# One reciprocal of four columns per head, one head later, in an attention and expert kernel

## The chip, the cores and the metric

The kernel runs on one core of one Trainium2 chip. The metric is the device time of one execution in microseconds (us); less is better. The median of 3 runs before the change is 1390.86 us (1388.47 to 1391.62). PE is the matrix engine (TensorE), DVE VectorE, ACT ScalarE, POOL or Pool GpSimd, SP the engine that issues most transfers.

## The reference

Four sequences x of 512 rows and 512 columns. First a layer norm and a product with a quantised context of 512 x 512, added to x. Then a transformer layer with a causal attention of 16 query heads and 4 key heads of 128 columns, and a mixture of 8 experts, 2 per row. What the change touches is the softmax of the attention:

```
h = rmsnorm(hidden, attn_norm_w)
q, k, v = h @ q_w.T, h @ k_w.T, h @ v_w.T        # 16, 4 and 4 heads of 128
q, k = apply_rope(rmsnorm(q, q_norm_w)), apply_rope(rmsnorm(k, k_norm_w))
scores = einsum('bhqd,bhkd->bhqk', q, k) * scale  # then the causal mask
attn = einsum('bhqk,bhkd->bhqd', softmax(scores, axis=-1), v)
hidden = hidden + attn @ o_w.T                    # then router and experts
```

## The kernel before

Two parts run one after the other: `mixer` (norms, context product, attention, preparation of the weights; until about 1056 us) and `moe` (router and experts). The change lies in the loop of `mixer` over 16 iterations `it` (four sequences times four key heads), each with G = 4 query heads h. A head is called (it, h) here, or by its running number s = 4 * it + h. The 512 query rows of a head are four blocks q of 128 rows; because of the causal mask block q has (q + 1) * 128 keys. The four blocks of a head lie side by side in a tile `prob`, of which there are three (LAG + 1, with LAG = 2).

The way of a block: PE computes the scores (`score`, L714 and L716, three products and the mask) into one of two banks; DVE scales them and takes the row maxima (`maxima`, L1291) into `prob`; ACT takes the exponentials with the row sums in `total` (`exponentials`, L960); DVE takes the reciprocal of the sums (`invert`, L1297) into `rtotal`; then blocks 0 to 2 are multiplied with it on Pool (`normalise`, L537) and block 3 on DVE (L1302). Two heads later PE transposes prob (`transpose_p`, L724), ACT copies the result to `pT` (L966) and PE multiplies with v (`values`, L735). ACT and DVE split that result in a high and a low part (`hi_attn` L974, `lo_attn` L1308) for the output product (`output`, L752). A score waits until DVE has read its bank two blocks before (`biased`). `transpose_p(s, 0)` waits for all three of Pool's blocks and for DVE's block 3 of head s.

Between these steps each engine does other work, written out by hand in the tables FILL, FRONT, ROUTE and SPLIT_*: a slot (h, place), with place 1 to 3, names units such as 'q' and 'kv' (projection of the next iteration, L680, its rope on DVE, L1254 to L1256, and on Pool, `add_rope`, L514), 'n' (`newton`, eleven small Pool operations), 'm', 'o' (output product of the iteration before), 'cm' (`column_maxima`, L500, a partition_all_reduce on Pool over maxima that DVE takes in L1142; in slot (1, 1) of iterations 3 and 7). `units(it, h, place)` gives them in the order of the tables, and each engine runs through its part of them in order; nothing overtakes on an engine.

Per head PE runs: scores 0 and 1, the units of place 1, transposes 0 and 1 of head s - 2, score 2, the units of place 2, values and transposes 2 and 3, score 3, values, the units of place 3. Pool's order is in `normalise` and the loop behind it (L564 to L579): scalings of blocks 0 and 1, the units of place 1, the scaling of block 2, the units of places 2 and 3. The order of DVE is at L1381 to L1395. In iterations 5, 9 and 13 `add_hidden` (L505), a transfer issued by Pool, stands ahead of the first head.

Of the kernel before, what the change touches and what calls it, by code (L numbers as in the profile page):

```python
# [15 lines left out]
ALU = mybir.AluOpType  # L16
# [6 lines left out]
TT = S // P  # L23
# [3 lines left out]
G = HQ // HKV  # L27
# [140 lines left out]
NIT = B * HKV  # L168
# [8 lines left out]
LAG = 2  # L177
# [36 lines left out]
def mixer(nc, x, ctxT, w_attn, wqkvo, wexp, wx_dram, qn, kn, cos, sin, w_ffn, gate_d, ident_d, mask_d, dispf_d, ident, logits, wcolf, extra, last_acc,  # L214
# [3 lines left out]
    with ExitStack() as ctx:  # L218
        def sb(name, shape, dt=F32):
            return ctx.enter_context(nc.sbuf_tensor(name, shape, dt))  # L220

        def sem(name):
            return ctx.enter_context(nc.semaphore(name))
# [4 lines left out]
        KEYS = [(q + 1) * P for q in range(TT)]  # L228
        P_AT = [sum(KEYS[:q]) for q in range(TT)]
# [19 lines left out]
        prob = [sb(f"prob{i}", [P, sum(KEYS)]) for i in range(LAG + 1)]  # L249
# [5 lines left out]
        bias, total, rtotal = sb("bias", [P, G * TT]), sb("total", [P, G * TT]), sb("rtotal", [P, G * TT])  # L255
# [38 lines left out]
        scored, biased, exp_done, inverted = sem("scored"), sem("biased"), sem("exp_done"), sem("inverted")  # L294
        prob_ready, prob3_ready, norm_seed, norm_done, pool_own = (sem(n) for n in ("prob_ready", "prob3_ready", "norm_seed", "norm_done", "pool_own"))
# [200 lines left out]
        @block.gpsimd  # L496
        def _(pool):
            def column_maxima(f):
                pool.wait_ge(camax_done, KC * (f + 1))
                nc.gpsimd.partition_all_reduce(camaxall[:, :], camax[:, :], P, bass.bass_isa.ReduceOp.max).then_inc(callmax_done, 1)  # L500

            def add_hidden(b):
                pool.wait_ge(x1_saved, 16 * TT * (b + 1))
                pool.wait_ge(o_added, TT * HKV * (b + 1))
                pool.dma_start(out[b * S:(b + 1) * S, :].rearrange("(t p) d -> p t d", p=P), acc[b % RING_X][:, :, :], accum_op=ALU.add).then_inc(hid_added, 16)  # L505

            def add_rope(j, t):

                if j == 0:
                    pool.wait_ge(kv_rotated, t + 1)  # L510
                    nc.gpsimd.tensor_tensor(r[:, t, G * HD:R], r[:, t, G * HD:R], rot[t % 2][:, G * HD:R], ALU.add).then_inc(rope_added, 1)
                    return
                pool.wait_ge(kv_rotated, TT * j + t + 1)
                nc.gpsimd.tensor_tensor(r[:, t, :], r[:, t, :], rot[t % 2][:, :], ALU.add).then_inc(rope_added, 1)  # L514

            def add_first(t):
                pool.wait_ge(q_rotated, t + 1)
                nc.gpsimd.tensor_tensor(r[:, t, 0:G * HD], r[:, t, 0:G * HD], rot[t % 2][:, 0:G * HD], ALU.add).then_inc(first_added, 1)

            def newton(j):  # L520

                own = Steps(pool, pool_own, 1 + NEWTON_STEPS * (j - 1))
                y, half = rn[:, :, :].rearrange("p t h -> p (t h)"), ssum[:, :, :].rearrange("p t h -> p (t h)")
                pool.wait_ge(norm_seed, j + 1)
                for i in range(3):
                    own.chain(nc.gpsimd.tensor_tensor(n1[:, :], y, y, ALU.mult))
                    own.chain(nc.gpsimd.tensor_tensor(n2[:, :], n1[:, :], half, ALU.mult))
                    own.chain(nc.gpsimd.tensor_tensor(n1[:, :], n15[:, :], n2[:, :], ALU.subtract))
                    if i < 2:
                        own.chain(nc.gpsimd.tensor_tensor(y, y, n1[:, :], ALU.mult))  # L530
                nc.gpsimd.tensor_tensor(y, y, n1[:, :], ALU.mult).then_inc(norm_done, 1)
                assert own.n == NEWTON_STEPS

            def normalise(it, h, q):
                pool.wait_ge(inverted, 16 * it + 4 * h + q + 1)
                p = prob[(G * it + h) % (LAG + 1)][:, P_AT[q]:P_AT[q] + KEYS[q]]
                nc.gpsimd.tensor_tensor(p, p, rtotal[:, 4 * h + q:4 * h + q + 1].broadcast_to([P, KEYS[q]]), ALU.mult).then_inc(prob_ready, 1)  # L537

            def tables():
                pool.wait_ge(table_in, 16 * 3)  # L540
                pool.wait_ge(const_in, 16 * 6)
                pool.wait_ge(cr_ready, KC)
                nc.gpsimd.tensor_copy(mask[:, :], mask_sb[:, :])
                nc.gpsimd.memset(zero, 0.0).then_inc(table_step, 1)
                pool.wait_ge(table_step, 1)
                for n in "qk":
                    nc.gpsimd.tensor_tensor(wneg[n], zero, hrow[n][:, H:HD], ALU.subtract).then_inc(table_step, 1)
                pool.wait_ge(table_step, 3)
                c3, s3 = cos_sb.rearrange("p (t h) -> p t h", h=H), sin_sb.rearrange("p (t h) -> p t h", h=H)
                for n in "qk":  # L550
                    for a in range(2):
                        sl = slice(a * H, (a + 1) * H)
                        other = hrow[n][:, 0:H] if a else wneg[n]
                        nc.gpsimd.tensor_tensor(tab[n, "c"][:, :, sl], c3, hrow[n][:, sl].unsqueeze(1).broadcast_to([P, TT, H]), ALU.mult).then_inc(table_step, 1)
                        nc.gpsimd.tensor_tensor(tab[n, "s"][:, :, sl], s3, other.unsqueeze(1).broadcast_to([P, TT, H]), ALU.mult).then_inc(table_step, 1)

            nc.gpsimd.memset(n15[:, :], 1.5).then_inc(pool_own, 1)
            tables()
            for t in range(TT):
                add_first(t)  # L560
            for t in range(TT):
                add_rope(0, t)
            column_maxima(1)
            for it in range(NIT):  # L564
                b, g = divmod(it, HKV)
                work = {"kv": lambda t: add_rope(it + 1, t), "n": lambda _: newton(it + 1), "cm": column_maxima}
                if g == 1 and b:
                    add_hidden(b - 1)
                for h in range(G):
                    normalise(it, h, 0)  # L570
                    normalise(it, h, 1)
                    for kind, i in units(it, h, 1):
                        if kind in work:
                            work[kind](i)
                    normalise(it, h, 2)
                    for place in (2, 3):
                        for kind, i in units(it, h, place):
                            if kind in work:
                                work[kind](i)  # L579
        @block.tensor  # L580
        def _(pe):
            def transposes_x(f, t, after=None):
# [186 lines left out]
            for it in range(NIT):  # L769
# [11 lines left out]
                for h in range(G):  # L781
                    s = G * it + h - LAG
# [294 lines left out]
        def _(dve):  # L1077
# [213 lines left out]
                nc.vector.tensor_scalar(prob[(G * it + h) % (LAG + 1)][:, P_AT[q]:P_AT[q] + KEYS[q]], bank[SC + q % 2][:, 0:KEYS[q]], nscale[it % 2][:, q, h:h + 1], None,  # L1291
                                        ALU.mult, ALU.min, accum_out=bias[:, n:n + 1]).then_inc(biased, 1)

            def invert(it, h, q):
                n = 4 * h + q
                dve.wait_ge(exp_done, 16 * it + n + 1)
                nc.vector.reciprocal(rtotal[:, n:n + 1], total[:, n:n + 1]).then_inc(inverted, 1)  # L1297
                if q == TT - 1:

                    dve.wait_ge(inverted, 16 * it + n + 1)  # L1300
                    p = prob[(G * it + h) % (LAG + 1)][:, P_AT[q]:P_AT[q] + KEYS[q]]
                    nc.vector.tensor_scalar(p, p, rtotal[:, n:n + 1], None, ALU.mult).then_inc(prob3_ready, 1)  # L1302

            def lo_attn(s):
                dve.wait_ge(at_hi, s + 1)
# [58 lines left out]
            for it in range(NIT):  # L1364
# [16 lines left out]
                for h in range(G):  # L1381
                    s = G * it + h - LAG
                    maxima(it, h, 0)
                    maxima(it, h, 1)
                    invert(it, h, 0)
                    invert(it, h, 1)
                    maxima(it, h, 2)
                    fill(h, 1)
                    invert(it, h, 2)
                    maxima(it, h, 3)  # L1390
                    fill(h, 2)
                    invert(it, h, 3)
                    if s >= 0:
                        lo_attn(s)
                    fill(h, 3)  # L1395
            def part_shift():
                dve.wait_ge(xp_done, NT)
                dve.wait_ge(lg_ready, NF)
                own.chain(nc.vector.tensor_reduce(pcol[0], logits[:, 0:NF, :], AX.X, ALU.max))
                nc.vector.tensor_tensor(part[0], logits[:, 0:NF, :], wide(pcol[0]), ALU.subtract).then_inc(shifted, 1)  # L1400
# [16 lines left out]
            def part_second():  # L1417
# [5 lines left out]
                for c in range(2):  # L1423
                    nc.vector.tensor_tensor(extra[:, 0:NF, 1 + c], pcol[1 + c], pcol[3], ALU.mult).then_inc(weighed, 1)

            part_shift()
            lo_attn(G * NIT - 2)
            part_first()
# [450 lines left out]
```

## Time and profile before

| | |
|---|---|
| median of 3 runs | 1390.86 us (1388.47 to 1391.62) |
| profiled execution | 1391.31 us, span 1389.5 us |
| mean granted clock of PE | 0.966 |
| PE busy | 1255.7 us, 90% |
| DVE busy | 842.7 us, 61% |
| ACT busy | 715.9 us, 52% |
| POOL busy | 384.9 us, 28% |
| L537, Pool's scalings | 192, 119.2 us busy, 626 ns each in the mean |
| L1291, DVE's maxima | 256, 134.9 us busy |

Busy times are those of one execution, whose own time is the one beside its span. A row of a timeline gives start, duration, engine, line, operation, output and inputs, the number of instructions merged into the row, and in square brackets the idle time before it with what ended it. "issue" stands where no releaser is seen. Times in the rows count from the start of the span.

### The profile page before, as it was taken

What the parts mean: (1) busy time and instruction counts of PE and PEld (TensorE: products, weight loads), DVE (VectorE), ACT (ScalarE), POOL (GpSimd) and SP (SyncE); (2) the same over time, 40 slices, a digit from 0 to 9 for tenths busy, and PEclk for the clock granted to TensorE, in tenths of its full rate; (3) what the DMA queues carried; (4) which work ended last, traced back from release to release, by engine and by line L of the source; (5) the groups of instructions that cost most, each with busy time, mean ns of one, the idle gap of its engine ahead of it and who ended that gap; (6) DMA issues with size and microseconds to landing.
All of it is one profiled execution on the core that took longest, in us unless ns stands there. A gap on an engine that the chain in (4) does not pass through costs nothing. (4 is left out here: it accounts for less than half of the span.)

```text
span 1389.5 us, 22860 instructions
## 1 busy us (share of the span) xinstructions
PE 1255.7 (90%) x6845; PEld 1012.8 (73%) x6845; DVE 842.7 (61%) x2480; ACT 715.9 (52%) x2290; POOL 384.9 (28%) x545
## 2 busy tenths in 40 slices
PE   1777899999999999989999999999996499999995
PEld 0466667778776777777767777878775498899995
DVE  7678776767886786578768665666644422222221
ACT  6447665565674566476656646556543033333331
POOL 0223121214322132322223233332210124333331
PEclk9988999999999999999999999999998699999998
DMA  3270335432355466738445664855304788877433
GB/s 99 75 283 28 121 107 183 174 129 92 152 165 178 161 212 200 250 113 243 166 158 188 209 204 151 264 194 184 104 4 133 277 318 218 247 211 205 77 62 38
DMA packets 89894, 228.50 MB, mean 164 GB/s; under 512 B 12272, under 2 KB 50032, under 8 KB 79536
## 3 DMA queue, kind: packets, MB, share of 16 engines
q1 hardware_dynamic: 63712, 184.03, 37.7%
q0 software_dynamic: 10848, 24.71, 9.8%
q10 hardware_dynamic: 15216, 18.30, 3.7%
q8 instruction: 60, 0.98, 0.3%
q14 instruction: 58, 0.48, 0.1%
HBM read 146.76 MB, written 80.24 MB: 163 GB/s over the span
## 5 line engine op out<-in xcount | busy, mean ns | idle before, releaser
L537 POOL TENSOR_TENSOR prob<-prob,rtotal 128x128 f32<-128x128 f32 (+2 forms) x192 | 119.2, 626 | 405.3 <-DVE rtotal L1297 379.0
L960 ACT ACTIVATE prob<-prob,bias 128x128 f32<-128x128 f32 (+3 forms) x256 | 145.1, 567 | 155.1 <-DVE prob L1291 154.3
L1291 DVE TENSOR_SCALAR_CACHE_REDUCE prob<-bank,nscale 128x128 f32<-128x128 f32 (+3 forms) x256 | 134.9, 546 | 147.1 <-PE bank L716 146.8
L735 PE MATMUL bank<-pT,v 128*128 128x512 f32 (+3 forms) x512 | 175.8, 445 | 9.0 <-ACT pT L966 8.3
L680 PE MATMUL bank<-w_hi,hT_hi 128*128 128x512 f32 x480 | 173.4, 361 | 4.1 <-DVE rot L1256 4.0
L966 ACT ACTIVATE pT<-bank 128x512 f32<-128x512 f32 (+3 forms) x256 | 102.9, 432 | 130.0 <-PE bank L724 129.8
L680 PE MATMUL bank<-w_hi,hT_lo 128*128 128x512 f32 x480 | 162.2, 338 | 0.0
L680 PE MATMUL bank<-w_lo,hT_hi 128*128 128x512 f32 x480 | 162.0, 337 | 0.0
L1602 PE MATMUL gu<-we,xT_hi 128*128 x624 | 156.5, 332 | 3.2 <-DVE xT_lo L1718 2.7
L514 POOL TENSOR_TENSOR r<-r,rot 128x640 f32<-128x640 f32 x60 | 99.3, 1655 | 196.1 <-DVE rot L1256 196.1
L714 PE MATMUL bank<-kT_hi,qT_hi 128*128 128x128 f32 (+3 forms) x256 | 101.8, 397 | 20.8 <-DVE prob L1291 20.8
L1602 PEld LDWEIGHTS gu<-we,xT_hi 128*128 128x128 f32 x624 | 109.3, 190 | 9.9 <-issue 7.9
L724 PEld LDWEIGHTS bank<-ident,prob 128*128 128x128 f32 x640 | 79.0, 143 | 47.6 <-issue 33.5
L752 PE MATMUL bank<-w_hi,aT_hi 128*128 128x512 f32 x256 | 107.4, 420 | 1.6 <-issue 1.6
L1580 POOL DMA_INDIRECT out<-y,ids x39 | 61.8, 1585 | 165.3 <-ACT y L1663 116.1
L724 PE MATMUL bank<-ident,prob 128*128 128x128 f32 x640 | 103.6, 277 | 0.0
L680 PEld LDWEIGHTS bank<-w_hi,hT_hi 128*128 128x128 f32 x480 | 91.9, 191 | 15.6 <-DVE rot L1256 8.0
L1602 PE MATMUL gu<-we,xT_lo 128*128 x312 | 101.8, 326 | 0.0
L752 PE MATMUL bank<-w_lo,aT_hi 128*128 128x512 f32 x256 | 101.3, 396 | 0.0
L752 PE MATMUL bank<-w_hi,aT_lo 128*128 128x512 f32 x256 | 101.2, 395 | 0.0
L735 PEld LDWEIGHTS bank<-pT,v 128*128 128x128 f32 x512 | 86.0, 193 | 20.4 <-ACT pT L966 8.7
L680 PEld LDWEIGHTS bank<-w_hi,hT_lo 128*128 128x128 f32 x480 | 91.0, 190 | 10.6
(312 smaller groups left out, 2852.9 us busy)
## 6 DMA issues: line engine op xcount, KB each, us to landing
w_hi<-ws_scratch SPq DMA_DIRECT2D x24, 1024.0 KB, 5.2
w_lo<-ws_scratch SPq DMA_DIRECT2D x24, 1024.0 KB, 7.8
we<-wx_scratch SPq DMA_DIRECT2D x16, 1408.0 KB
we<-wx_scratch SPq DMA_DIRECT2D x16, 768.0 KB, 10.9
stage<-in_wexp SPq DMA_DIRECT2D x64, 176.0 KB, 2.4
wx_scratch<-ehi ACTq DMA_DIRECT2D x64, 176.0 KB, 2.0
wx_scratch<-stage SPq DMA_DIRECT2D x64, 176.0 KB, 2.5
stage<-in_wqkvo SPq DMA_DIRECT2D x40, 256.0 KB, 3.6
```

Of the source, the lines that this page charges most:

```text
L514: nc.gpsimd.tensor_tensor(r[:, t, :], r[:, t, :], rot[t % 2][:, :], ALU.add).then_inc(rope_added, 1)
L537: nc.gpsimd.tensor_tensor(p, p, rtotal[:, 4 * h + q:4 * h + q + 1].broadcast_to([P, KEYS[q]]), ALU.mult).then_inc(prob_ready, 1)
L680: last = nc.tensor.matmul(o, hT[a][:, k, t * P:(t + 1) * P], wkv(j, c, k) if kv else wq(j, c, k), start=(k == 0 and n == 0), stop=(k == KC ...
L714: nc.tensor.matmul(o[:, 0:KEYS[q]], qT[a][:, h, q * P:(q + 1) * P], kT[it % 2][c][:, 0:KEYS[q]], start=(n == 0), stop=False)
L724: last = nc.tensor.transpose(bank[PT + j % 2][:, (q - j) * P:(q - j + 1) * P], prob[s % (LAG + 1)][:, P_AT[q] + j * P:P_AT[q] + (j + 1) * ...
L735: nc.tensor.matmul(bank[PV][:, j * P:S], v[it % (LAG + 1)][:, j, :], pT[:, PT_AT[j]:PT_AT[j] + QS[j]], start=(j == 0), stop=(j == TT - 1)) ...
L752: last = nc.tensor.matmul(bank[t % 2][:, :], aT[a][:, (G * o + h) % RING_A, t * P:(t + 1) * P], wo(c, h), start=(h == 0 and n == 0), stop= ...
L960: nc.scalar.activation(p, p, ACT.Exp, bias=bias[:, 4 * h + q:4 * h + q + 1], scale=-1.0, accum_out=total[:, 4 * h + q:4 * h + q + 1]).then ...
L966: nc.scalar.activation(pT[:, PT_AT[j]:PT_AT[j] + QS[j]], bank[PT + j % 2][:, 0:QS[j]], ACT.Copy).then_inc(pt_copied, 1)
L1291: nc.vector.tensor_scalar(prob[(G * it + h) % (LAG + 1)][:, P_AT[q]:P_AT[q] + KEYS[q]], bank[SC + q % 2][:, 0:KEYS[q]], nscale[it % 2][:, ...
L1580: pool.indirect_dma_start(out, bass.IndirectOffsetOnAxis(ap=ids[:, i:i + 1], axis=0), y[i % 3][:, :], None, compute_op=ALU.add).then_inc(y ...
L1602: last = nc.tensor.matmul(gu[i % 2][u][:, 0:I], xT[a][i % 2][:, k, :], we[:, bass.ds(at + (c * ECOLS + k * GU + u * I), I)], start=(k == 0 ...
```

## The change

DVE takes the reciprocals of a head's four row sums in one operation of four columns, in the head after, behind its maxima 1; the scaling of block 3 goes with it. Pool's three scalings of a head move to the head after as well, in the same places of the order. The last head is handled behind the loop.

```diff
@@ Pool, loop over the heads
                 for h in range(G):
-                    normalise(it, h, 0)
-                    normalise(it, h, 1)
+                    s = G * it + h - 1
+                    if s >= 0:
+                        normalise(s // G, s % G, 0)
+                        normalise(s // G, s % G, 1)
                     for kind, i in units(it, h, 1):
                         if kind in work:
                             work[kind](i)
-                    normalise(it, h, 2)
+                    if s >= 0:
+                        normalise(s // G, s % G, 2)
                     for place in (2, 3):
                         for kind, i in units(it, h, place):
                             if kind in work:
                                 work[kind](i)
+            for q in range(TT - 1):
+                normalise(NIT - 1, G - 1, q)
@@ DVE
-            def invert(it, h, q):
-                n = 4 * h + q
-                dve.wait_ge(exp_done, 16 * it + n + 1)
-                nc.vector.reciprocal(rtotal[:, n:n + 1], total[:, n:n + 1]).then_inc(inverted, 1)
-                if q == TT - 1:
-
-                    dve.wait_ge(inverted, 16 * it + n + 1)
-                    p = prob[(G * it + h) % (LAG + 1)][:, P_AT[q]:P_AT[q] + KEYS[q]]
-                    nc.vector.tensor_scalar(p, p, rtotal[:, n:n + 1], None, ALU.mult).then_inc(prob3_ready, 1)
+            def invert(s):
+                it, h = divmod(s, G)
+                n, q = 4 * h, TT - 1
+                dve.wait_ge(exp_done, 4 * s + TT)
+                nc.vector.reciprocal(rtotal[:, n:n + TT], total[:, n:n + TT]).then_inc(inverted, TT)
+                dve.wait_ge(inverted, 4 * s + TT)
+                p = prob[s % (LAG + 1)][:, P_AT[q]:P_AT[q] + KEYS[q]]
+                nc.vector.tensor_scalar(p, p, rtotal[:, n + q:n + q + 1], None, ALU.mult).then_inc(prob3_ready, 1)
@@ DVE, loop over the heads
                     maxima(it, h, 0)
                     maxima(it, h, 1)
-                    invert(it, h, 0)
-                    invert(it, h, 1)
+                    if G * it + h:
+                        invert(G * it + h - 1)
                     maxima(it, h, 2)
                     fill(h, 1)
-                    invert(it, h, 2)
                     maxima(it, h, 3)
                     fill(h, 2)
-                    invert(it, h, 3)
                     if s >= 0:
                         lo_attn(s)
                     fill(h, 3)
@@ DVE, behind the loop
+            invert(G * NIT - 1)
             part_shift()
             lo_attn(G * NIT - 2)
             part_first()
```

## Rows read from the trace of the kernel before

**Rows 1.** The page, busy time of each engine (share of the span), instructions.
```profile
PE 1255.7 (90%) x6845; PEld 1012.8 (73%) x6845; DVE 842.7 (61%) x2480; ACT 715.9 (52%) x2290; POOL 384.9 (28%) x545
```
**Rows 2.** Waits of PE, 92 to 1045 us: total us, times, longest.
```profile
PE bank L714 <- DVE prob L1291: 20.8, 20, 4.3
...
PE bank L704 <- DVE kT_lo L1313: 5.8, 3, 5.2
PE bank L680 <- DVE rot L1256: 4.0, 10, 0.6
PE bank L634 <- DVE logits L1232: 3.8, 3, 2.2
```
**Rows 3.** Lines L1297 and L1302: duration ns minimum/median/maximum.
```profile
L1297 DVE RECIPROCAL rtotal<-total x256: 146/164/167, 94.1 to 1037.7; 128x1 f32<-128x1 f32 x128
L1302 DVE TENSOR_SCALAR prob<-prob,rtotal x64: 485/487/1590, 104.0 to 1037.9; 128x512 f32<-128x512 f32 x64
```
**Rows 4.** Timeline of DVE, maxima 3 to scaling of head (5,2).
```profile
430.61 0.75 DVE L1291 TENSOR_SCALAR_CACHE_REDUCE prob<-bank,nscale 128x512 f32<-128x512 f32 x1 [3.98 <-PE bank L716]
...
436.10 0.15 DVE L1297 RECIPROCAL rtotal<-total 128x1 f32<-128x1 f32 x1
436.29 0.49 DVE L1302 TENSOR_SCALAR prob<-prob,rtotal 128x512 f32<-128x512 f32 x1
```
**Rows 5.** Timeline of PE, score 2 of head (5,3).
```profile
440.62 0.45 PE L714 MATMUL bank<-kT_hi,qT_hi 128*128 128x384 f32 x1 [1.70 <-DVE prob L1291]
```
**Rows 6.** Timeline of DVE, maxima 1 of head (15,0).
```profile
997.25 0.48 DVE L1291 TENSOR_SCALAR_CACHE_REDUCE prob<-bank,nscale 128x256 f32<-128x256 f32 x1
```
**Rows 7.** Timeline of PE, transposes in head (15,1).
```profile
1003.47 0.94 PE L724 MATMUL bank<-ident,prob 128*128 128x128 f32 x7
```
**Rows 8.** Timeline of DVE, last output addition in the loop.
```profile
1040.46 0.69 DVE L1318 TENSOR_TENSOR last_acc<-bank,last_acc 128x512 f32<-128x512 f32 x1 [1.29 <-PE bank L752]
```
**Rows 9.** Timeline of PE, transposes of the last head.
```profile
1044.40 0.93 PE L724 MATMUL bank<-ident,prob 128*128 128x128 f32 x7
```
**Rows 10.** Timeline of Pool, `add_hidden` in iteration 5.
```profile
387.80 1.59 POOL L505 DMA_DIRECT2D out<-last_acc  x1 [4.40 <-DVE last_acc L1318]
```
**Rows 11.** Timeline of Pool around the reduction of iteration 3.
```profile
294.51 1.12 POOL L537 TENSOR_TENSOR prob<-prob,rtotal 128x128 f32<-128x128 f32 x2 [3.42 <-DVE rtotal L1297]
296.79 1.57 POOL L514 TENSOR_TENSOR r<-r,rot 128x640 f32<-128x640 f32 x1 [1.16 <-DVE rot L1256]
304.50 0.39 POOL L500 PARTITION_ALL_REDUCE camaxall<-camax  x1 [6.14 <-issue]
312.75 0.82 POOL L537 TENSOR_TENSOR prob<-prob,rtotal 128x384 f32<-128x384 f32 x1 [7.86 <-issue]
```
**Rows 12.** Timeline of DVE, the maxima that the reduction waits for.
```profile
296.62 2.28 DVE L1142 TENSOR_REDUCE camax<-cb 128x16 f32<-128x2048 f32 x1
```
**Rows 13.** Timeline of PE, transposes in heads (3,2) and (3,3).
```profile
305.66 0.93 PE L724 MATMUL bank<-ident,prob 128*128 128x128 f32 x7
...
318.28 0.93 PE L724 MATMUL bank<-ident,prob 128*128 128x128 f32 x7
```
**Rows 14.** Timeline of Pool around the reduction of iteration 7.
```profile
546.21 0.39 POOL L500 PARTITION_ALL_REDUCE camaxall<-camax  x1 [6.58 <-issue]
554.01 0.86 POOL L537 TENSOR_TENSOR prob<-prob,rtotal 128x384 f32<-128x384 f32 x1 [7.41 <-issue]
```
**Rows 15.** Timeline of PE, transposes in head (7,2).
```profile
548.30 0.93 PE L724 MATMUL bank<-ident,prob 128*128 128x128 f32 x7
```
**Rows 16.** Windows: us, busy PE, PEld, DVE, ACT, POOL, granted clock, DMA.
```profile
145.00:148.50 3.50, 1.06 (x6) 1.07 (x6) 2.97 (x6) 2.41 (x6) 0.00 (x0) 0.52 1.00 412
148.50:152.00 3.50, 3.50 (x19) 3.41 (x18) 1.81 (x8) 2.51 (x7) 0.86 (x2) 0.50 1.03 386
```
**Rows 17.** Timeline of PE, one matmul of L752 at each clock.
```profile
436.17 0.39 PE L752 MATMUL bank<-w_hi,aT_hi 128*128 128x512 f32 x1
...
443.73 0.63 PE L752 MATMUL bank<-w_lo,aT_hi 128*128 128x512 f32 x1
```

## The prediction

> **What bounds the kernel now.** I read the busy shares first: PE 90%, DVE 61%, POOL 28% [rows 1]. DVE and Pool, on which the change works, are therefore no bound by themselves; their work counts only where PE waits for it. The second view is the list of PE's waits in the attention loop (92 to 1045 us) [rows 2]. The reader is to see how little there is to win: 20.8 us in 20 waits of a score matmul (L714) for DVE's maxima, 5.8 for kT_lo, 4.0 for rot, 3.8 for the logits, and not one wait of a transpose of prob (L724). So the scaled prob is always there in time today, and the question is whether it still is when it comes a head later.
>
> **What it removes.** Per head, three of four one-column reciprocals, 256 x 164 ns before [rows 3], 64 after (I price a four-column one like a one-column one: the issue of such a tiny operation dominates; the bounds are 0.16 and twice that, nothing either way). That is 192 x 0.16 = 31 us of DVE time, and the waits for the exponentials of the same head go too. The scaling of block 3 (0.487 us) stays, but moves from behind `fill(h, 2)` to behind `maxima(h+1, 1)`. What of this PE feels is read in the streak before a typical wait [rows 4]: DVE runs without a break from maxima 3 of head (5,2) to maxima 0 of head (5,3), and in this streak lie one reciprocal and the scaling; from 436.10 to the end of the scaling at 436.78 they take 0.7; where the streak holds a second reciprocal, 0.9. PE had stood for 1.70 and starts at 440.62 as soon as DVE's block 0 is through [rows 5]. Behind the change such a wait is 0.7 to 0.9 shorter. Of the 20 waits ten are 0.66 us or longer and make 16.2 of the 20.8; one of them is ACT's doing, which leaves 9 x 0.7 = 6.3; the ten short ones lose little (1); the waits for rot and the logits lie behind the same DVE work and give perhaps 1.5. What is late next is ACT's `hi_attn`, which `lo_attn` waits for anyway, and ACT's dequantisation. Sum -8.8; I take **-8**, since one DVE streak serves several waits in a row. Bounds: -2 (only the clearest three) and -14 (all of L704 and L634 too).
>
> Between maxima 1 and maxima 2 little changes: today DVE takes two reciprocals there and stands for the exponentials ahead of each; afterwards one reciprocal and the scaling fill 0.7. I take 0; bounds -0.2 and +0.7 per head of DVE time, which PE feels only in the waits priced above. Nothing is queued behind `exp_done` there that was not before, since the exponential of block 3 of the previous head is long through.
>
> **What it adds: a head less of slack, and a place in Pool's queue.** Pool scales blocks 0 to 2 of head s now in head s+1, and PE reads all of prob(s) in head s+2, behind place 1. In an ordinary head that is enough: Pool's first scaling in head (3,1) starts at 294.51, after the change that is head (3,0)'s, and PE reads it at 305.66 [rows 11, 13], 11.1 us later, while the scalings take 1.12 and 0.82 and one rope addition 1.57. The tightest are the last two iterations: maxima 1 of head (15,0) starts at 997.25 and PE transposes at 1003.47 [rows 6, 7], 5.7 us behind its end, for a need of 0.16 + 1.12 + 0.82 and perhaps 0.5 that Pool waits beside DVE's scaling, 2.6. At the end DVE's last `invert` stands behind the output addition that starts at 1040.46 and lasts 0.69 [rows 8], so it runs at about 1041.2, Pool is through by 1043.8, and PE wants it at 1044.40 [rows 9]. Cost 0; bounds 0 and 1.5. `add_hidden` now stands ahead of the previous head's scalings in Pool's queue, with 1.59 us [rows 10] against over 10 of slack; its wait for `o_added` ends ahead of the reciprocal that the scaling waits for. Nothing on SP's queue moves.
>
> One place is different. In slot (1,1) of iterations 3 and 7 Pool also has `column_maxima`, the partition_all_reduce, and it stands **between the scalings of blocks 0, 1 and of block 2**. Follow Pool in iteration 3 [rows 11]: rope addition at 296.79, then 6.14 idle ("issue", no releaser), the reduction at 304.50, which lasts 0.39, then 7.86 idle, again "issue", and at 312.75 the scaling of block 2. DVE's maxima of the context that feed it end at 298.90 (296.62 + 2.28) [rows 12]. So Pool is shut for 13.9 us. Today the block behind it belongs to head (3,1), read at 318.28, so the hole is hidden with 4.7 to spare. After the change it is block 2 of head **(3,0)**, and PE turns to that head's prob at 305.66 [rows 13]. Pool is done at 312.75 + 0.82 = 313.6. PE, with some 0.1 for the signal, stands for **8.0 us**. In iteration 7 the reduction is at 546.21 and the scaling at 554.01 + 0.86 = 554.9 [rows 14], PE's transposes at 548.30 [rows 15]: **6.7 us**. The hole itself doesn't move, since DVE and ACT feed it from before the stall. It is PE that stops, and all that it computes is needed, so 14.7 are lost. From the second some 0.7 may come back, as the wait for the logits just behind it (the longest of [rows 2], 2.2) arises from Pool's backlog beside DVE. I take **+14**; bounds 11 and 16. Behind each stall nothing else is late: Pool catches up while PE stands.
>
> The clock. A wait of 5.2 us [rows 2] ends at 147.4 (148.5 less the 1.06 us busy); the granted clock is 0.52 in 145.0 to 148.5 and 0.50 in 148.5 to 152.0 [rows 16], its lower level of 1.2 GHz, so 4.6 us after work resumed were at half clock. A matmul of 512 columns then takes 0.63 in place of 0.39 [rows 17]: a microsecond there loses between 0.38 (by these durations) and 0.5 (by the two levels). Two stalls of this kind lose 2 x 4.6 x 0.44 = **+4**; bounds +1 and +9 (twice the stretch). Some half-clock stretches behind the short waits may go; I take -0.5 for them, bounds 0 and -4.
>
> **Sum.** -8 + 14 + 4 - 0.5 = +9.5. The profiled execution took 1391.3 (span 1389.5), 0.4 above the median of 1390.86. So 1391.3 + 9.5 = 1400.8 for such an execution, 1400.4 for the median: slower by 0.7%.
>
> **Rivals.** *A: Pool isn't shut after the reduction.* The page says that spans on POOL are rough, and the 7.86 behind the reduction have no releaser. If they were the tail of something that today's order happens to allow, block 2 could be scaled as soon as the reduction is through. The point from which it decides: block 2 of head (3,0) starts before about 305. Then there is no stall, and no half clock behind one: 1391.3 - 8 - 0.5 = 1382.8. For it: nothing in the trace names what Pool does there. Against it: the next instruction had all it needed long before, twice, with nearly the same idle time (7.86 and 7.41) [rows 11, 14]. Chance 0.05.
> The Trainium skill's page "GPSIMD Engine Reference", section "Instruction dispatch", says that the first call of a freshly loaded kernel pays about 6 us of code load. By that alone the hole would be 6 us once and PE would hardly stand; the trace agrees for the way in (298.90 to 304.50), but shows a second, longer hole on the way back, and the measured hole decides.
>
> *B: DVE and Pool get in each other's way.* The scaling of block 3 takes 487 ns at the median and 1590 at most [rows 3], the long ones beside a Pool operation already running. After the change it runs each time beside Pool's first scaling. If each pays 1.10, the 0.85 that a late head saves at best turns into 0.25 lost, and 20 waits grow by 5 us in place of shrinking by 8: 1391.3 + 14 + 4 + 5 = 1414. Against it: DVE starts the scaling 0.19 behind the start of the reciprocal [rows 4], while Pool must first see the signal, so DVE should be first and Pool pay. Chance 0.08. The Trainium skill's "GPSIMD Engine Reference", section "Key points", states that Pool shares its SBUF interfaces with DVE and names the two-port mode; it doesn't say who waits.
>
> *C: the relief is the larger part.* DVE's streaks shorten so much that ACT and PE run closer (-14) and half-clock stretches go (-4), with the stalls at their lower bound (+11) and short clock loss (+3): 1391.3 - 4 = 1387. Chance 0.04.
>
> *D: the stalls are hidden or halved* (Pool reaches the reduction earlier since DVE is less loaded): +7, +2, -8: 1392. Against it: what the reduction waits for lies in the same head on DVE, behind PE's own scores, so it comes forward no more than PE does. Chance 0.05.
>
> **Chances.** The forecast 0.78. Its own spread: low -13 + 12 + 1 - 1 = -1, high -3 + 16 + 9 = +22, but not all at once: +3 to +17. With B at +23 the range is 1393 to 1409; it leaves out A, C, D and half of B, 0.18. Slower by over 0.2% (2.8 us, about what a measurement of this kernel tells from no change): 0.77 + 0.08 = 0.85; within 0.2%: D and 0.01 of the forecast's lower end, 0.06; faster: A and C, 0.09.
>
> **What would show it.** Right: PE waits of 6 to 8 us before L724, released by Pool's L537, in iterations 3 and 7, and none elsewhere; the granted clock at half behind them; Pool's block 2 of heads (3,0) and (7,0) directly behind the 7 to 8 us hole; PE's waits for L1291 down from 20.8 to 12 or so; DVE busy down by some 31. Wrong: no L724 wait, or L1302 with a median well over 0.5 (B), or L1291 waits unchanged or under 8.

## The result, and the profile after

The changed kernel takes 1401.42 us at the median of 7 runs (1396.8 to 1405.42), the kernel before 1390.86 (1388.47 to 1391.89, 7 runs): ratio 1.0079, 95% interval 1.0066 to 1.0093, so 9 to 13 us slower. The forecast was 1400.4, in a range of 1393 to 1409. The profiled execution of the changed kernel has a span of 1400.4 us, 10.9 above that of before.

The first row to read is the busy time of each engine on the profile's page, against [rows 1]:

```profile
PE 1256.0 (90%) x6845; PEld 1012.9 (72%) x6845; DVE 829.9 (59%) x2288; ACT 716.8 (51%) x2290; POOL 392.7 (28%) x545
```

DVE has 192 instructions and 12.8 us less, and the kernel is slower all the same. PE's waits (92 to 1060 us of the changed kernel; total, times, longest) answer to [rows 2]; line numbers have moved by five, behind `invert` by four:

```profile
PE bank L719 <- DVE prob L1296: 19.5, 18, 5.6
PE bank L729 <- POOL prob L537: 14.8, 2, 7.8
PE bank L740 <- ACT pT L971: 7.4, 10, 2.5
PE bank L709 <- DVE kT_lo L1317: 5.5, 2, 5.3
PE bank L685 <- DVE rot L1261: 3.0, 7, 0.6
PE bank L757 <- issue: 1.6, 1, 1.6
PE bank L639 <- DVE logits L1237: 1.2, 3, 0.4
```

The second row is new: PE's transposes of prob wait for Pool, twice, 14.8 us in all. Every other total is the same or smaller: over the same window all rows of before sum to 45.4 us and all of these, with two more of 0.6 and 0.5, to 54.1, so the other waits fell by 6.1 (the logits 2.6, the maxima 1.3, rot 1.0, pT 0.9, kT_lo 0.3). Where the two new waits are is in Pool's timeline around the reduction of iteration 3 (answers to [rows 11]) and of iteration 7 ([rows 14]):

```profile
295.69 1.16 POOL L537 TENSOR_TENSOR prob<-prob,rtotal 128x128 f32<-128x128 f32 x2 [3.55 <-DVE rtotal L1303]
298.20 1.57 POOL L514 TENSOR_TENSOR r<-r,rot 128x640 f32<-128x640 f32 x1 [1.36 <-DVE rot L1261]
305.61 0.39 POOL L500 PARTITION_ALL_REDUCE camaxall<-camax  x1 [5.83 <-issue]
314.14 0.82 POOL L537 TENSOR_TENSOR prob<-prob,rtotal 128x384 f32<-128x384 f32 x1 [8.14 <-issue]
...
555.06 0.67 POOL L500 PARTITION_ALL_REDUCE camaxall<-camax  x1 [6.76 <-issue]
563.27 0.82 POOL L537 TENSOR_TENSOR prob<-prob,rtotal 128x384 f32<-128x384 f32 x1 [7.54 <-issue]
```

and PE starts as soon as block 2 is scaled (timeline of PE, to [rows 13, 15]):

```profile
315.01 1.76 PE L729 MATMUL bank<-ident,prob 128*128 128x128 f32 x7 [7.78 <-POOL prob L537]
...
564.14 1.75 PE L729 MATMUL bank<-ident,prob 128*128 128x128 f32 x7 [7.02 <-POOL prob L537]
```

The seven transposes take 1.76 in place of 0.93 us, at a granted clock of 0.50: PE comes back at its lower level. Windows behind the two stalls (us, busy PE, PEld, DVE, ACT, POOL, granted clock, DMA share, GB/s):

```profile
315.00:319.60 4.60, 4.59 (x20) 4.28 (x21) 1.70 (x5) 2.83 (x12) 3.17 (x4) 0.50 0.00 0
319.60:323.00 3.40, 3.40 (x18) 2.22 (x17) 0.37 (x2) 1.18 (x5) 0.00 (x0) 1.00 0.51 134
...
564.10:568.80 4.70, 4.66 (x20) 4.35 (x21) 1.77 (x5) 3.19 (x13) 3.21 (x4) 0.50 0.00 0
```

PE is busy throughout at half clock, 4.6 and 4.7 us, as behind the 5.2 us wait of [rows 16]. Yet PE's busy time over the whole kernel is that of before, 1256.0 against 1255.7 us, with as many matmuls. Half clock has gone elsewhere. The kernel before has, among others, three such stretches at about 442, 561 and 814 us (they fill most of these windows, not all):

```profile
440.00:444.00 4.00, 3.38 (x12) 2.71 (x13) 3.46 (x12) 3.40 (x11) 2.46 (x8) 0.77 0.87 294
560.00:564.00 4.00, 2.76 (x14) 2.60 (x15) 1.92 (x8) 1.07 (x2) 2.89 (x12) 0.70 0.98 406
814.00:818.00 4.00, 3.87 (x16) 3.53 (x17) 1.42 (x6) 1.87 (x5) 2.62 (x11) 0.57 0.98 402
```

In the changed kernel the clock is full in the same work a little later (450 to 458 and 824 to 832 us), the one at 561 has given way to the one behind the stall, and one is new at 248. In steps of 1 us from 92 to 1045, PE worked 26 us at half clock before and 25 after.

DVE's side shows in the wait that the prediction followed, [rows 4, 5]. Timeline of PE in the changed kernel, score 2 of head (5,3):

```profile
451.16 0.45 PE L719 MATMUL bank<-kT_hi,qT_hi 128*128 128x384 f32 x1 [1.12 <-DVE prob L1296]
```

1.70 has become 1.12. The scaling of block 3 (duration in ns, minimum/median/maximum, to [rows 3]) has got longer, the reciprocal of four columns hardly, against 164 ns for one column:

```profile
L1303 DVE RECIPROCAL rtotal<-total x64: 166/172/177, 108.5 to 1050.1; 128x4 f32<-128x4 f32 x64
L1306 DVE TENSOR_SCALAR prob<-prob,rtotal x64: 485/727/1129, 108.7 to 1050.3; 128x512 f32<-128x512 f32 x64
```

### The profile page after: what moved, and what is told of

It reads as the page before. It is cut to its first block and busy times, and to the rows that moved or that the text cites. A ratio compares the mean times of both kernels' runs of the same rounds, so it can differ in the third digit from the quotient of the medians.

```text
span 1400.4 us, 22732 instructions
## 1 busy us (share of the span) xinstructions
PE 1256.0 (90%) x6845; PEld 1012.9 (72%) x6845; DVE 829.9 (59%) x2288; ACT 716.8 (51%) x2290; POOL 392.7 (28%) x545
## 5 line engine op out<-in xcount | busy, mean ns | idle before, releaser
L537 POOL TENSOR_TENSOR prob<-prob,rtotal 128x128 f32<-128x128 f32 (+2 forms) x192 | 126.6, 683 | 273.1 <-DVE rtotal L1303 257.5
L719 PE MATMUL bank<-kT_hi,qT_hi 128*128 128x128 f32 (+3 forms) x256 | 101.6, 397 | 19.8 <-DVE prob L1296 19.5
L729 PE MATMUL bank<-ident,prob 128*128 128x128 f32 x640 | 104.8, 279 | 14.8 <-POOL prob L537 14.8
```

The lines of the kernel that those rows point to most:

```text
L719: nc.tensor.matmul(o[:, 0:KEYS[q]], qT[a][:, h, q * P:(q + 1) * P], kT[it % 2][c][:, 0:KEYS[q]], start=(n == 0), stop=False)
L729: last = nc.tensor.transpose(bank[PT + j % 2][:, (q - j) * P:(q - j + 1) * P], prob[s % (LAG + 1)][:, P_AT[q] + j * P:P_AT[q] + (j + 1) * ...
```

## The experiments

The kernels were timed in three groups, each beside its own executions of the kernel before: the first four rows, the next four, the last three. Ratios are to those, with 95% intervals; the last column is the difference of the medians. Across groups only ratios are compared. The lists of waits and busy times are of one profiled execution each.

| kernel | median us | before us | ratio | difference |
|---|---|---|---|---|
| block 2 first | 1377.73 | 1388.45 | 0.9918 (0.9897 to 0.9939) | -10.7 |
| only the reduction moved | 1382.96 | 1388.45 | 0.9962 (0.9948 to 0.9976) | -5.5 |
| Pool a head later only | 1409.39 | 1388.45 | 1.0142 (1.0122 to 1.0163) | +20.9 |
| third reduction | 1407.08 | 1388.45 | 1.0124 (1.0101 to 1.0147) | +18.6 |
| before, reduction late | 1394.23 | 1387.61 | 1.0044 (1.0029 to 1.0060) | +6.6 |
| scaling 3 behind maxima 2 | 1382.22 | 1387.61 | 0.9953 (0.9940 to 0.9966) | -5.4 |
| four reciprocals | 1377.90 | 1387.61 | 0.9926 (0.9913 to 0.9940) | -9.7 |
| copy for the reduction | 1379.39 | 1387.61 | 0.9937 (0.9924 to 0.9950) | -8.2 |
| scaling 3 behind maxima 3 | 1391.60 | 1389.69 | 1.0014 (1.0003 to 1.0026) | +1.9 |
| block 2 first, again | 1376.79 | 1389.69 | 0.9912 (0.9893 to 0.9931) | -12.9 |
| changed kernel, again | 1397.31 | 1389.69 | 1.0058 (1.0038 to 1.0079) | +7.6 |

**Take Pool's block 2 out from behind the hole.** On Pool, in the changed kernel:

```diff
+                    if s >= 0:
+                        normalise(s // G, s % G, 2)
                     for kind, i in units(it, h, 1):
                         if kind in work:
                             work[kind](i)
-                    if s >= 0:
-                        normalise(s // G, s % G, 2)
```

> The changed kernel, but Pool scales block 2 ahead of the units of place 1 in every head, so neither the reduction nor a rope addition stands between the scaling of a head and PE's reading of it. My theory (the loss is two stalls of PE, 7.8 and 7.0 us, behind the reduction's hole, plus the half clock behind them, and DVE's relief of some 5 us is real): no wait of L724 for Pool, 1401.4 - 14.8 - 3 = 1383 to 1387, faster than the kernel before by 4 to 7 us. Rival B (DVE and Pool in each other's way, scaling of block 3 at 727 ns in place of 487): the time stays above 1395 though the stalls are gone. Rival 'relief is nothing': 1390 to 1392.

0.9918, and 0.9912 in the third group: the fastest kernel of all here. Timeline of Pool in iteration 3: all three blocks, then the rope addition, then a hole as before.

```profile
296.10 1.94 POOL L537 TENSOR_TENSOR prob<-prob,rtotal 128x128 f32<-128x128 f32 x3 [3.51 <-DVE rtotal L1303]
298.61 1.56 POOL L514 TENSOR_TENSOR r<-r,rot 128x640 f32<-128x640 f32 x1 [0.57 <-DVE rot L1261]
306.22 0.39 POOL L500 PARTITION_ALL_REDUCE camaxall<-camax  x1 [6.06 <-issue]
315.37 1.55 POOL L514 TENSOR_TENSOR r<-r,rot 128x640 f32<-128x640 f32 x1 [8.76 <-DVE rot L1261]
```

PE's transposes are there at 307.49 without a wait. With the stalls the loss is gone, and the price of rival B is out. But the gain is 10.7 us, where I expected 4 to 7. This edit moves two things from ahead of block 2, the hole and the rope addition; the next kernel takes them apart.

**Move only the reduction.** In the changed kernel the units of place 1 run in their old place, except 'cm', which comes behind block 2:

```diff
-                    for kind, i in units(it, h, 1):
-                        if kind in work:
+                    held = [(kind, i) for kind, i in units(it, h, 1) if kind in work]
+                    for kind, i in held:
+                        if kind != "cm":
                             work[kind](i)
                     if s >= 0:
                         normalise(s // G, s % G, 2)
+                    for kind, i in held:
+                        if kind == "cm":
+                            work[kind](i)
```

> The changed kernel, but only the reduction of slot (1,1) in iterations 3 and 7 is moved behind the scaling of block 2; the rope additions stay ahead of it. If only the hole costs: the same as the kernel with block 2 first in every head, within 1.5 us (1383 to 1387). If the order of rope addition and block 2 matters to DVE (which waits for rope additions) the two differ by 2 us or more.

0.9962. Against the changed kernel's 1.0079 the two holes cost 1.2% or 16 us, against the 1.0058 of its second measurement 13 (forecast 18). Against the kernel with block 2 first it is 5.2 us slower: the rope addition ahead of block 2 costs too. One place is to be seen in iteration 2, head (2,1), of the changed kernel, which has the same order there. Pool's timeline, then DVE's:

```profile
238.61 1.57 POOL L514 TENSOR_TENSOR r<-r,rot 128x640 f32<-128x640 f32 x1 [1.50 <-DVE rot L1261]
240.13 0.83 POOL L537 TENSOR_TENSOR prob<-prob,rtotal 128x384 f32<-128x384 f32 x1
```
```profile
238.85 1.36 DVE L1181 TENSOR_SCALAR var<-mv 128x4 f32<-128x4 f32 x1
240.25 0.75 DVE L62 TENSOR_SCALAR t<-var 128x4 uint32<-128x4 uint32 x1
```

Two operations on 4 columns end just behind the end of a Pool operation each (240.18 and 240.96): they seem to wait for it. With block 2 first the second one doesn't:

```profile
242.87 0.17 DVE L62 TENSOR_SCALAR t<-var 128x4 uint32<-128x4 uint32 x1
```

and the wait of PE behind it is 0.47 in place of 1.06 us. Summed over PE's waits in the loop, without the row "issue", the profiles differ by 4.8 us (38.9 and 34.1). The spans of these two executions differ by 2.0 only, since PE's busy time is 1.6 lower in the slower one (1251.7 and 1253.3), so how the 5.2 us come about is shown in part.

**Pool later, DVE as before.** This is the kernel before with Pool's loop of the change; DVE's code is untouched.

> The kernel before, with Pool's scalings a head later as in the change, but DVE's four reciprocals and its scaling of block 3 where they were. My theory: both stalls (about 8.0 and 6.7 us) and the half clock behind them, without DVE's relief: 1390.9 + 14 + 3.5 = 1406 to 1410, that is 5 to 8 us above the changed kernel, and PE's waits for maxima at 19 to 21 us. If DVE's relief is worth nothing: 1401, as the changed kernel. If the change's DVE part costs (rival B): below 1400.

1.0142, and 1409.39 us lies in the expected range. It has the same two stalls, of 7.4 and 5.3 us, and none of DVE's relief. PE's waits for maxima are 23.5 us, above the 19 to 21 that I expected (PE's waits in its loop):

```profile
PE bank L719 <- DVE prob L1296: 23.5, 20, 6.2
PE bank L729 <- POOL prob L537: 12.7, 2, 7.4
```

The changed kernel lies under it by 0.6% (1.0079) to 0.8% (1.0058) of the kernel before: with Pool a head later, DVE's part of the change gains 9 to 12 us.

**One more stall.** In the changed kernel, on Pool behind the units of place 1:

```diff
+                    if (it, h) == (11, 1):
+                        nc.gpsimd.partition_all_reduce(camaxall[:, :], camax[:, :], P, bass.bass_isa.ReduceOp.max)
```

> The changed kernel with one more partition_all_reduce in slot (1,1) of iteration 11, whose result nobody reads. My theory: a third stall there. Pool's hole of 13.4 to 13.9 us begins at the end of the rope addition; from the rows of the kernel before PE would stand 5 to 6 us, and 1.5 to 2.5 us go to the half clock: 1401.4 + 7.5, range +5 to +9. If a stall is absorbed by waits further on: under +3.

1.0124, that is 6.2 us over the changed kernel by its first ratio and 9 by its second. PE's timeline:

```profile
821.31 1.76 PE L731 MATMUL bank<-ident,prob 128*128 128x128 f32 x7 [5.73 <-POOL prob L537]
```

The stall is paid. Of its half clock (4.2 us of work behind it) the totals can't say so much: in the profiles the spans differ by 6.6, PE's waits for Pool by 5.2, the other waits fall by 2.8, and PE's busy time grows by 5.0, more than the 2 us or so that this stretch costs. Half clock came up in other places too.

**Control: the reduction late in the kernel before.**

```diff
-                    for kind, i in units(it, h, 1):
-                        if kind in work:
+                    held = [(kind, i) for kind, i in units(it, h, 1) if kind in work]
+                    for kind, i in held:
+                        if kind != "cm":
                             work[kind](i)
                     normalise(it, h, 2)
+                    for kind, i in held:
+                        if kind == "cm":
+                            work[kind](i)
```

> Control: the kernel before, with the reduction of slot (1,1) moved behind that head's scaling of block 2 and nothing else. My theory: the hole is hidden in the kernel before in either order, so 0, within 2 us of it. If the hole cost something there already (Pool's backlog beside DVE, the wait for the logits), up to 3 us faster.

A miss: 1.0044, slower by 6.6 us. In the kernel before, block 2's reciprocal comes late in the head. So the hole begins at 300.2 (299.39 + 0.83), and it is longer here (Pool's timeline):

```profile
299.39 0.83 POOL L537 TENSOR_TENSOR prob<-prob,rtotal 128x384 f32<-128x384 f32 x1 [2.51 <-DVE rtotal L1301]
306.16 0.39 POOL L500 PARTITION_ALL_REDUCE camaxall<-camax  x1 [5.94 <-issue]
318.44 1.56 POOL L514 TENSOR_TENSOR r<-r,rot 128x640 f32<-128x640 f32 x1 [11.88 <-issue]
```

Behind it stand two rope additions and `newton`, whose result DVE needs for k, and PE's turn to wait comes later:

```profile
327.71 1.54 PE L708 MATMUL bank<-ident,r 128*128 128x128 f32 x6 [3.19 <-DVE r L1289]
```

This wait and the 3.0 us of half clock behind it make some 4.7 us (an estimate: 3.2 and half of 3.0); the spans of the profiled executions differ by 4.1. So the hole holds up two users, prob and k, and in the kernel before neither of them made PE wait. The rest of the 6.6 us is open.

**Where the scaling of block 3 stands.** In the kernel with block 2 first, the reciprocal stays behind maxima 1, the scaling goes behind maxima 2:

```diff
                         invert(G * it + h - 1)
                     maxima(it, h, 2)
+                    if G * it + h:
+                        scale3(G * it + h - 1)
```

> The kernel with block 2 first, and DVE's scaling of block 3 behind maxima 2 in place of ahead of it. In the changed kernel that scaling takes 727 ns at the median where it took 487, beside Pool's scalings. If DVE is held up there where PE waits: 1 to 3 us faster than the kernel with block 2 first. My theory: that place is not on PE's path, so within 1 us of it, whatever the median of the scaling becomes.

A miss: 0.9953 against 0.9918 and 0.9912, so 5 to 6 us slower than with block 2 first. In the profiles PE's waits in the loop are 2.7 us more, in many small ones. PE's busy time is 1.7 more, with a stretch of half clock (3.4 us) at 248 that the changed kernel has too and the one with block 2 first has not. What makes these waits I did not trace.

In these two kernels `invert` issues the reciprocal alone, `scale3` the scaling. The scaling behind maxima 3 instead, in the stretch in which DVE is late:

```diff
                     maxima(it, h, 3)
+                    if G * it + h:
+                        scale3(G * it + h - 1)
                     fill(h, 2)
```

> The kernel with block 2 first, and DVE's scaling of block 3 (still a head later) behind maxima 3, that is back in the stretch between maxima 3 and maxima 0 in which DVE is late for PE. My theory (DVE's relief is the 0.5 us scaling and the reciprocals out of that stretch): PE's waits for maxima and logits grow by 0.5 each in nine to eleven places, so 4 to 6 us slower than the kernel with block 2 first in this call, waits for maxima back to 20 us or so. If the place of the scaling is nothing and only the waits for exponentials counted: within 1 us of it.

> The kernel with block 2 first once more, as the yardstick of this call: 0.992 of the kernel before, 0.990 to 0.994, PE's waits for maxima at 16 to 18 us.

1.0014 against 0.9912 in the same group: 14.8 us, three times what I expected. PE's waits in its loop; the kernel with block 2 first has 16.4 in 18, 2.4 in 7 and no other row that differs by more than 0.7:

```profile
PE bank L719 <- DVE prob L1296: 22.0, 20, 6.0
PE bank L685 <- DVE rot L1261: 8.3, 19, 1.0
```

I had counted nine to eleven waits for maxima and logits; twelve more waits for rot appear, nine more than the kernel before has (10, [rows 2]). The place is not quite the old one, which may be why: in the kernel before the scaling stood behind `fill(h, 2)`, with rot's products ahead of it, here it stands in front of them. DVE in head (2,1) of the kernel before:

```profile
247.30 0.41 DVE L1256 TENSOR_TENSOR rot<-bank,tab_q_s 128x256 f32<-128x256 f32 x1
247.63 0.15 DVE L1297 RECIPROCAL rtotal<-total 128x1 f32<-128x1 f32 x1
247.82 0.49 DVE L1302 TENSOR_SCALAR prob<-prob,rtotal 128x512 f32<-128x512 f32 x1
```

So the 14.8 us are the price of this place, and what the old one costs by itself no kernel here shows. And this kernel's scaling is the quick one:

```profile
L1309 DVE TENSOR_SCALAR prob<-prob,rtotal x64: 476/483/726, 113.4 to 1042.5; 128x512 f32<-128x512 f32 x64
```

487 ns in the mean, where it is 700 with block 2 first: 14 us less of DVE work, and 14.8 us more of time. The place decides here, not the duration.

**Merging or moving.** In the kernel with block 2 first:

```diff
-                nc.vector.reciprocal(rtotal[:, n:n + TT], total[:, n:n + TT]).then_inc(inverted, TT)
+                for c in range(TT):
+                    nc.vector.reciprocal(rtotal[:, n + c:n + c + 1], total[:, n + c:n + c + 1]).then_inc(inverted, 1)
```

> The kernel with block 2 first, but four reciprocals of one column in place of one of four, at the same place a head later. It separates the merging from the moving. My theory: the three extra ones (some 0.1 to 0.2 us each, 20 to 38 us of DVE in all) lie between maxima 1 and 2 where PE seldom waits: +0 to +2 us. If the number of DVE instructions is what counts: +5 us or more, nearly all of the 10.7 us gain given back.

0.9926 against 0.9918 and 0.9912. The intervals overlap: one reciprocal of four columns is worth 0 to 2 us, and the rest of the gain is the move to the next head.

**No reduction, same place.** In the changed kernel `column_maxima` of iterations 3 and 7 becomes a copy. This leaves out the maximum over the partitions.

```diff
-                nc.gpsimd.partition_all_reduce(camaxall[:, :], camax[:, :], P, bass.bass_isa.ReduceOp.max).then_inc(callmax_done, 1)
+                nc.gpsimd.tensor_copy(camaxall[:, :], camax[:, :]).then_inc(callmax_done, 1)
```

> The changed kernel, but in iterations 3 and 7 Pool copies its input of the reduction instead of reducing it over the partitions, in the same slot and order (this leaves out the maximum over the partitions, so the scales of the context differ). It tells whether it is the hole around the reduction and not a Pool operation in that place as such. My theory: no wait of L729 for Pool, 15 to 18 us faster than the changed kernel, that is 5 to 7 us faster than the kernel before, as with the reduction moved. Rival: the place in the queue is enough to stall PE; then 5 us faster than the changed kernel at most.

0.9937, which is 17 to 20 us under the changed kernel, and no wait of PE for Pool. A Pool operation in that place of the queue makes no stall without the hole. By the medians it is 3.5 us faster than with the reduction moved (the intervals just touch). A reason fits: PE's wait for the logits, 1.82 in iteration 7 of that kernel, is 0.41 here, and the half clock behind it (0.55 in 556.3 to 560.0 there) is full clock here.

**The changed kernel once more.**

> The changed kernel once more in the same call: 1.0079 of the kernel before, 1.0065 to 1.0093, so 21 to 24 us above the kernel with block 2 first; two waits of PE for Pool of 7 to 8 us.

1.0058 (1.0038 to 1.0079), a little under the first measurement and under what I expected; the intervals overlap. The two stalls are 7.9 and 6.0 us, the second again under the expected 7 to 8. The median lies 20.5 us above the kernel with block 2 first in the same group.

## Why the prediction was right

The path that makes the kernel slower, the two stalls, was right. The terms of the sum were less so, and that it came out within 2 us is in part luck: errors of opposite sign cancel. In the profiled executions (span 10.9 us above before):

| term | forecast | in the profiles |
|---|---|---|
| DVE's relief, as waits of PE | -8 | -6.1 |
| two stalls | +14 | +14.8 |
| half clock, behind the stalls and elsewhere | +4 - 0.5 | +0.3 (PE's busy time) |
| not in the waits of the loop | 0 | +1.9 |
| sum | +9.5 | +10.9 |

**The stalls.** 8.0 and 6.7 us were forecast, 7.78 and 7.02 measured, in the two heads that were named, and no other head waits for Pool. Over the nine stalls of the four profiled executions that have them they were 5.3 to 7.9. That they are the cause is shown by the kernel in which only the reduction moved and by the one with the copy. In the first PE's only wait for Pool is 0.3 us, in the second there is none. The third reduction adds one.

**The clock.** +4 was forecast for 4.6 us at the lower level behind each stall, and 4.6 and 4.7 were measured; behind all nine it was 4.0 to 5.7, with no order by the length of the wait (5.7 behind one of 6.0, 4.6 behind one of 7.8). The step that failed is the other term: the half-clock stretches behind short waits were to give back 0.5 (bounds 0 and -4). PE's busy time grew by 0.3, so they gave back nearly all of the 4. How much of that is the change's doing stays open, since such stretches differ between kernels that are otherwise close: PE's busy time is 1251.7 with the reduction moved, 1247.6 with the copy, and 1253.3 and 1252.5 in two executions with block 2 first.

**DVE's relief.** -8 was taken from bounds -2 and -14. The pairs give -5.5 (reduction moved against before) and -9 to -12 (changed against Pool-later-only), so the size is about right. Its place is not. The row for maxima was to fall from 20.8 to 12 or so and went to 19.5, nearly unchanged, which the prediction had named as a sign of being wrong. The largest part is the logits' (3.8 to 1.2 us), which it had priced at 1.5 together with rot. Five of the long waits for maxima did shrink by about 0.6 (1.70 to 1.12 here), but others grew: the long one of head (0,2) went from 4.34 to 5.64 though PE's score came 0.65 earlier, and one at 600 us from 1.08 to 1.67. A wait's length says when the waiting engine came, too. The count of waits was also off: eleven are 0.66 us or longer and make 18.0 us, not ten with 16.2; the one left out (1.87 at 93.65) did not shrink.

What I got wrong in it is the sort of gain. I priced it by waits that existed. With the scaling between maxima 3 and rot's products the kernel takes 14.8 us more for half a microsecond per head, much of it in waits for rot that weren't there. And merging the reciprocals, the 31 us of DVE work that I wrote down, is worth 0 to 2 us. DVE's busy time fell by 12.8 only. By the sums of single durations the reciprocals fell by 30.2 (41.2 to 11.0), the scaling grew by 6.3 (38.4 to 44.7) and some small operations by the rest, 20.6 less in all (950.1 to 929.5). Neighbouring operations overlap, and the busy time (842.7 to 829.9) counts an overlap once.

**Ends of slack.** The last two iterations and the end of the loop cost nothing, as forecast: no transpose waits there, and PE's last waits of the loop are those of before.

**The rivals.** A (no second half of the hole) is out: it was 6.9 to 11.9 us long behind every reduction in iterations 3, 7 and 11. B was half right as a mechanism and wrong in its price: the scaling does get longer beside Pool (487 to 727 ns at the median, the second of the prediction's signs of being wrong that came up; 600 to 698 in the mean). But it does so between maxima 1 and 2, and the kernel in which it is quick again in the other place is the slower one. C and D fall with the measured stalls. The Trainium skill's figure of about 6 us of code load at the first call of a freshly loaded kernel (page "GPSIMD Engine Reference", section "Instruction dispatch") agrees with the 5.8 to 6.9 us from Pool's last operation to the reduction in iterations 3, 7 and 11 of all profiled kernels. Here it is paid each time, not once, and what the page doesn't state is the way back. The 13.9 us of the prediction begin at the end of DVE's maxima; the load doesn't seem to wait for them, as the rows at the end of this document show.

## What to carry to other kernels

When a step is moved by one turn of a loop, follow it past every rare item in each queue, not only past those of an ordinary turn: two reductions in 64 heads turned a gain of 5 us into a loss of 8 to 11, and one step moved ahead turned it into a gain of 11 to 13. Price half a microsecond on an engine by where it stands: in the stretch in which another engine is nearly held up it cost 15 us here, and three more small instructions per head elsewhere 0 to 2. Test a hidden cost from both sides, since the control that was to cost nothing cost 6.6 us. And check a forecast by its terms: PE's total busy time showed at once that the clock had cost nothing net, which the windows behind the stalls alone hide.

## What was not expected of the hardware

The idle time of Pool around a partition_all_reduce is marked in the trace, which the prediction overlooked when it said that nothing names what Pool does there. The queue of Pool records MODIFY_POOL_CONFIG in the kernel before (answers for L500 and L537; duration in ns, first and last start):

```profile
L500 POOLq MODIFY_POOL_CONFIG  x6: 10/16/28, 83.0 to 539.9; - x6
L537 POOLq MODIFY_POOL_CONFIG  x6: 88/88/88, 89.0 to 546.6; - x6
```

The last of the first row stands at 539.9, right behind the rope addition (which ends at 539.63) and before DVE's maxima are there (540.19); the last of the second stands at 546.6, at the end of the reduction (546.21 + 0.39). In the kernel with the copy L500 has two such records, both at 84 us, and none of the holes in iterations 3 and 7. At the first reduction the way in seems to have run while Pool waited for DVE: the record stands at 83.0, DVE's maxima end at 88.53 and the reduction starts at 88.66.

The idle time of Pool behind a partition_all_reduce, up to its next ordinary operation, differs from kernel to kernel: 6.9 to 8.2 us mostly, but 8.8, 9.1, 9.7 and 11.9 in iteration 3 of four kernels (at the end of the 8.8 the profile names a wait for DVE's rot). In the longest case the DMA engines were saturated in that time (windows of the control with the reduction late; clock, DMA share and GB/s at the end):

```profile
310.00:314.00 4.00, 4.00 (x25) 3.40 (x23) 3.44 (x13) 1.30 (x3) 0.00 (x0) 1.00 0.98 390
314.00:318.00 4.00, 4.00 (x24) 3.40 (x23) 1.05 (x7) 1.53 (x6) 0.00 (x0) 1.00 1.06 398
```

Over all profiled kernels the holes with a DMA share of 0.34 to 0.45 (iterations 7 and 11) took 6.9 to 7.6 us, those with 0.92 to 1.00 (iteration 3) 7.5 to 11.9. That the way back waits behind these transfers fits, but it is not shown: no run here takes the transfers away, and with nearly the same share the holes lie between 7.5 and 9.7.
